# Writing the turned query weights back in the third row block of the next group, in 2 KB pieces, with the order of all lists written anew

## The reference, cut to what matters

```python
x = x + attn(layernorm(x), Wq, Wk, Wv, Wo, q_norm_w, k_norm_w)   # 32 heads, causal, alibi, q and k RMS-normalised
x = x + ffn(layernorm(x), A, B, Wr, br)                          # softmax router over 8 low-rank experts
# attn, per group g: q = x Wq[g].T, k = x Wk[g].T, v = x Wv[g].T
# scores = q k.T / sqrt(128) + slope * rel (causal); p = softmax(scores); o = p v; y += o Wo[:, g].T
```

## Time and profile before

| | |
|---|---|
| median of 3 runs | 2138.23 us (2137.99 to 2138.62) |
| the profiled execution's own time | 2138.16 us |
| its span, first to last instruction | 2136.3 us |
| granted PE clock, mean | 0.993 of full speed |
| PE busy | 2083.0 us, 98% of the span |
| DVE, ACT, POOL busy | 63%, 54%, 44% |
| DMA | 176.81 MB, mean 83 GB/s |
| queue of SP, queue of ACT | 72.41 MB in 305264 packets, 102.25 MB in 23664 |

### The profile page before, as it was taken

How to read it: one execution, slowest core, us unless ns; L and a number is a source line. 1 busy time by engine, 2 the same in 40 slices (tenths; PEclk the granted TensorE clock), 3 DMA queues, 4 the chain that set the end, 5 groups by cost and what they waited for, 6 DMA issues and landing times.

```text
span 2136.3 us, 33509 instructions
## 1 busy us (share of the span) xinstructions
PE 2083.0 (98%) x11772; PEld 1786.4 (84%) x11772; DVE 1355.6 (63%) x3431; ACT 1148.2 (54%) x3314; POOL 936.1 (44%) x984
## 2 busy tenths in 40 slices
PE   7999999999999999999999999999999999999997
PEld 6888888888888888888888888888888888888885
DVE  6656656566565665658876556566566656656676
ACT  4555545555454654645445555555555555555552
POOL 3443434444444443444443544435453443545443
PEclk9999999999999999999999999999999999999998
DMA  4152141511415125051350422313041231304112
GB/s 158 64 140 75 30 130 64 154 60 40 133 54 150 60 55 157 16 154 55 110 157 7 113 70 68 101 50 92 28 107 62 67 102 50 89 30 106 44 36 73
DMA packets 329095, 176.81 MB, mean 83 GB/s; under 512 B 243800, under 2 KB 301144, under 8 KB 320736
## 3 DMA queue, kind: packets, MB, share of 16 engines
q1 hardware_dynamic: 305264, 72.41, 15.3%
q10 hardware_dynamic: 23664, 102.25, 12.8%
HBM read 99.11 MB, written 75.50 MB: 82 GB/s over the span
## 4 chain that ended last, share of the span: by engine, by line
PE 83%; DVE 4%; issue 4%; DMA 3%; SPq 2%; POOL 2%; ACT 2%; ACTq 0%; DVEq 0%; POOLq 0%
PE s_ps L1026 17%; PE q_ps L1026 15%; PE y_ps L1026 15%; PE o_ps L1026 15%; PE turn_ps L1113 13%; PE turn_ps L1026 5%; DMA p_raw<-p_bounce 3%; SPq L568 2%; POOL probs_odd L799 1%; PE turn_ps L1107 1%; PE y_ps L1186 1%; DVE pT_lo L898 1%; DMA p_bounce<-probs_odd 1%; DVE y L955 0%; DVE oT_lo L949 0%
## 5 line engine op out<-in xcount | busy, mean ns | idle before, releaser
L799 POOL TENSOR_TENSOR probs_odd<-probs_odd,p_inv 128x256 f32<-128x256 f32 (+3 forms) x256 | 316.4, 1256 | 326.9 <-DVE p_inv L928 326.9
L706 ACT ACTIVATE pT_hi<-turn_ps 128x512 fp32r<-128x512 f32 x464 | 271.6, 597 | 316.2 <-PE turn_ps L1113 315.9
L799 POOL TENSOR_TENSOR probs_even<-probs_even,p_inv 128x128 f32<-128x128 f32 (+3 forms) x256 | 261.8, 1044 | 386.1 <-DVE p_inv L928 386.1
L898 DVE TENSOR_TENSOR pT_lo<-turn_ps,pT_hi 128x512 fp32r<-128x512 f32 x464 | 314.6, 684 | 146.2 <-ACT pT_hi L706 145.2
L921 DVE CUSTOM_DVE_ANT_0 probs_odd<-s_ps,rel 128x256 f32<-128x256 f32 (+3 forms) x256 | 209.3, 820 | 131.9 <-issue 131.4
L1026 PE MATMUL s_ps<-kT_hi,qT_hi 128*128 128x512 f32 (+3 forms) x768 | 278.7, 363 | 2.6 <-DVE kT_lo L900 1.8
L1026 PE MATMUL s_ps<-kT_hi,qT_lo 128*128 128x512 f32 (+3 forms) x768 | 262.9, 342 | 0.0
L1026 PE MATMUL s_ps<-kT_lo,qT_hi 128*128 128x512 f32 (+3 forms) x768 | 262.1, 341 | 0.0
L720 ACT ACTIVATE probs_odd<-probs_odd,neg_max 128x256 f32<-128x256 f32 (+3 forms) x256 | 211.9, 832 | 76.0 <-DVE neg_max L921 75.9
L921 DVE CUSTOM_DVE_ANT_0 probs_even<-s_ps,rel 128x128 f32<-128x128 f32 (+3 forms) x256 | 174.0, 686 | 118.0 <-issue 117.2
L1026 PE MATMUL o_ps<-pT_hi,v_hi 128*128 128x512 f32 x576 | 243.9, 423 | 1.9 <-DVE pT_lo L898 0.9
(11 more groups left out here) (110 smaller groups left out, 4578.6 us busy)
## 6 DMA issues: line engine op xcount, KB each, us to landing
p_raw<-p_bounce SPq DMA_DIRECT2D x448, 64.0 KB, 2.3
p_bounce<-probs_odd SPq DMA_DIRECT2D x64, 256.0 KB, 2.3
wq_kept<-wqT_hi ACTq DMA_DIRECT2D x8, 1024.0 KB, 5.8
wq_kept<-wqT_lo ACTq DMA_DIRECT2D x8, 1024.0 KB, 8.4
wo_kept<-woT_hi ACTq DMA_DIRECT2D x8, 1024.0 KB, 8.1
wo_kept<-woT_lo ACTq DMA_DIRECT2D x8, 1024.0 KB, 10.2
p_bounce<-probs_even SPq DMA_DIRECT2D x64, 128.0 KB, 1.8
wqT_hi<-wq_kept ACTq DMA_DIRECT2D x8, 1024.0 KB, 4.8
```

The source lines that it names most:

```text
L706: nc.scalar.activation(target, bank, ACT.Copy).then_inc(sems["high"], 1)
L799: nc.gpsimd.tensor_tensor(row, row, p_inv[:, s % 2, h:h + 1].to_broadcast((P, L)), ALU.mult).then_inc(sems["normalise"], 1)
L898: nc.vector.tensor_tensor(target, bank, upper.bitcast(F32), ALU.subtract).then_inc(sems["low"], 1)
```

## The change

Three things are edited. The kept copies of all turned weights get another layout in HBM, in which a run is 2 KB rather than 8 KB (4 KB for the keys' and values'). `keep_wq(w)` now means the weights of group w itself. And all six lists are replaced by others with the same operations; only `keep_wq` leaves `PROLOGUE` and is added to `BOUNDARY`. The order of the operations on every engine changes with them, in many places. In `GROUP_A` the DMA issues stand so:

| issue on ACT's queue | before, behind | after, behind |
|---|---|---|
| `load_wq` | `max.2.1` | `max.2.3` |
| `keep_wq` | `values.7.1` | `scores.4.0` (ACT: `high.p.2.2`) |
| `load_wkv` | `flip_p.6.6` | `max.4.2` |
| `keep_wo` | `exp.2.0` | `values.4.3` (ACT: `square_q.7`) |
| `load_wo` | `high.p.7.1` | `normalise.6.2` (ACT: `high.p.5.4`) |
| `keep_wkv` | `values.7.3` | `turn.k.0` (ACT: `upper_p.7.6`) |

```diff
-        wq_kept = nc.dram_tensor("wq_kept", [NG, 2, P, C * W512], F32).ap()
+        wq_kept = nc.dram_tensor("wq_kept", [NG, 2, C, P, W512], F32).ap()
...
+        def pieces(kept, g, part):
+            return kept[g, part].rearrange("c p n -> p c n")
+
+        def pairs(turned):
+            return turned[:].rearrange("p (a c) n -> p a (c n)", c=2).bitcast(F32)
...
             def keep_wq(w):
-                after(act, "low", "wq", w + 1, C - 1)
-                act.dma_start(wq_kept[w + 1, 0], wqT_hi[:].rearrange("p c n -> p (c n)").bitcast(F32)).then_inc(wq_spilled, 16)
-                act.dma_start(wq_kept[w + 1, 1], wqT_lo[:].rearrange("p c n -> p (c n)").bitcast(F32)).then_inc(wq_spilled, 16)
+                after(act, "low", "wq", w, C - 1)
+                act.dma_start(pieces(wq_kept, w, 0), wqT_hi[:].bitcast(F32)).then_inc(wq_spilled, 16)
+                act.dma_start(pieces(wq_kept, w, 1), wqT_lo[:].bitcast(F32)).then_inc(wq_spilled, 16)
```

`keep_wo`, `keep_wkv` and the three `back_` functions are changed in the same way. The end of `GROUP_A` after:

```diff
+    "fetch_p.7.5 values.6.3 add_y.5 values.6.4 fetch_p.7.6 values.6.5 turn.p.7.0 values.6.6 high.p.7.0 turn.p.7.1 "
...
+    "values.7.4 flip_p.7.7 values.7.5 upper_p.7.6 turn.k.0 keep_wkv lower_p.7.6 y.6 upper_p.7.7 high.k.0 lower_p.7.7 "
```

More of the change, by code:

```diff
@@ L480, in x_normed @@
             return x_source(b, t)
-        wkv_kept = nc.dram_tensor("wkv_kept", [NG, 2, P, C * 2 * HD], F32).ap()
-        wq_kept = nc.dram_tensor("wq_kept", [NG, 2, P, C * W512], F32).ap()
-        wo_kept = nc.dram_tensor("wo_kept", [NG, 2, P, G * DM], F32).ap()
+        wkv_kept = nc.dram_tensor("wkv_kept", [NG, 2, C // 2, P, W512], F32).ap()
+        wq_kept = nc.dram_tensor("wq_kept", [NG, 2, C, P, W512], F32).ap()
+        wo_kept = nc.dram_tensor("wo_kept", [NG, 2, G, P, DM], F32).ap()
+        def pieces(kept, g, part):
+            return kept[g, part].rearrange("c p n -> p c n")
+        def pairs(turned):
+            return turned[:].rearrange("p (a c) n -> p a (c n)", c=2).bitcast(F32)
         p_bounce = nc.dram_tensor("p_bounce", [2, NT, G, P, P], F32).ap()
@@ L630, in keep_wkv @@
                 after(act, "low", "wkv", w + 1, 1)
-                act.dma_start(wkv_kept[w + 1, 0], wkvT_hi[:].rearrange("p c n -> p (c n)").bitcast(F32)).then_inc(wkv_spilled, 16)
-                act.dma_start(wkv_kept[w + 1, 1], wkvT_lo[:].rearrange("p c n -> p (c n)").bitcast(F32)).then_inc(wkv_spilled, 16)
+                act.dma_start(pieces(wkv_kept, w + 1, 0), pairs(wkvT_hi)).then_inc(wkv_spilled, 16)
+                act.dma_start(pieces(wkv_kept, w + 1, 1), pairs(wkvT_lo)).then_inc(wkv_spilled, 16)
             def keep_wq(w):
-                after(act, "low", "wq", w + 1, C - 1)
-                act.dma_start(wq_kept[w + 1, 0], wqT_hi[:].rearrange("p c n -> p (c n)").bitcast(F32)).then_inc(wq_spilled, 16)
-                act.dma_start(wq_kept[w + 1, 1], wqT_lo[:].rearrange("p c n -> p (c n)").bitcast(F32)).then_inc(wq_spilled, 16)
+                after(act, "low", "wq", w, C - 1)
+                act.dma_start(pieces(wq_kept, w, 0), wqT_hi[:].bitcast(F32)).then_inc(wq_spilled, 16)
+                act.dma_start(pieces(wq_kept, w, 1), wqT_lo[:].bitcast(F32)).then_inc(wq_spilled, 16)
             def keep_wo(w):
                 after(act, "low", "wo", w, G - 1)
-                act.dma_start(wo_kept[w, 0], woT_hi[:].rearrange("p c n -> p (c n)").bitcast(F32)).then_inc(wo_spilled, 16)
-                act.dma_start(wo_kept[w, 1], woT_lo[:].rearrange("p c n -> p (c n)").bitcast(F32)).then_inc(wo_spilled, 16)
+                act.dma_start(pieces(wo_kept, w, 0), woT_hi[:].bitcast(F32)).then_inc(wo_spilled, 16)
+                act.dma_start(pieces(wo_kept, w, 1), woT_lo[:].bitcast(F32)).then_inc(wo_spilled, 16)
             def back_wkv(w):
@@ L647, in back_wkv @@
                 act.wait_ge(wkv_spilled, 32 * NG)
-                act.dma_start(wkvT_hi[:].rearrange("p c n -> p (c n)").bitcast(F32), wkv_kept[g, 0]).then_inc(wkv_back, 16)
-                act.dma_start(wkvT_lo[:].rearrange("p c n -> p (c n)").bitcast(F32), wkv_kept[g, 1]).then_inc(wkv_back, 16)
+                act.dma_start(pairs(wkvT_hi), pieces(wkv_kept, g, 0)).then_inc(wkv_back, 16)
+                act.dma_start(pairs(wkvT_lo), pieces(wkv_kept, g, 1)).then_inc(wkv_back, 16)
             def back_wq(w):
@@ L654, in back_wq @@
                 act.wait_ge(wq_spilled, 32 * NG)
-                act.dma_start(wqT_hi[:].rearrange("p c n -> p (c n)").bitcast(F32), wq_kept[g, 0]).then_inc(wq_back, 16)
-                act.dma_start(wqT_lo[:].rearrange("p c n -> p (c n)").bitcast(F32), wq_kept[g, 1]).then_inc(wq_back, 16)
+                act.dma_start(wqT_hi[:].bitcast(F32), pieces(wq_kept, g, 0)).then_inc(wq_back, 16)
+                act.dma_start(wqT_lo[:].bitcast(F32), pieces(wq_kept, g, 1)).then_inc(wq_back, 16)
             def back_wo(w):
@@ L661, in back_wo @@
                 act.wait_ge(wo_spilled, 32 * NG)
-                act.dma_start(woT_hi[:].rearrange("p c n -> p (c n)").bitcast(F32), wo_kept[g, 0]).then_inc(wo_back, 16)
-                act.dma_start(woT_lo[:].rearrange("p c n -> p (c n)").bitcast(F32), wo_kept[g, 1]).then_inc(wo_back, 16)
+                act.dma_start(woT_hi[:].bitcast(F32), pieces(wo_kept, g, 0)).then_inc(wo_back, 16)
+                act.dma_start(woT_lo[:].bitcast(F32), pieces(wo_kept, g, 1)).then_inc(wo_back, 16)
             def high(w, of, *which):
```

## The result

The kernel after takes 2108.43 us (median of 4 runs, 2108.18 to 2110.02); the kernel before, run beside it on the same chip, 2138.43 (2137.99 to 2139.65). The ratio is 0.986, 95% interval 0.9843 to 0.9877: 30.0 us less. The forecast was 25.1 less, 2113.1.

The account below looks back on a forecast made before the run. PE, busy 98% of the span, bounds the kernel; only its idle time and slow clock can be won. 25.4 - 1.0 + 1.5 - 0.8 = 25.1 us less than 2138.16 gives 2113.1 us, range 2105 to 2127.

Parts of the forecast that it names:

- Step 1, the six A periods: GROUP_A periods: y.6 no longer waits for add_y.5 behind slow fetches; 131.4 to 127.9 us each, 21.0 us saved.
- Either edit alone would take this wait away: Moving the transfers, or moving add_y.5 ahead of row 7's flips, would each end y.6's wait in GROUP_A.
- the fourth rival: Flip's place on DVE, not the collision, caused the wait; same 25 us gain, chance included in the forecast's 0.74.
- Step 1, group 0: Group 0, ahead of the first y.7: wait of 2.6 and slow product's 1.8 give 4.4 us saved.
- Step 2, what is late next in A: Values 7.7 have some 3 us slack; thinner places in the seven A groups cost 1 us, bounds 0 to 7.
- Step 3, the issues that moved: keep_wq about 34 us into the group, keep_wo at 67, load_wo at 80: their new places cost nothing.
- Step 4, pieces of 2 KB: Kept copies in 2 KB runs: charged 0, bounds 0 to 2 us a group of batch 1.
- Step 5, batch 1 and the seams: Six GROUP_B periods save 1.5 us at y.7; prologue, boundary, first batch 1 and last groups lose 0.8, bounds -5 to +5.
- half of it: Row 7 chain late at the A groups' end, PE waits about 1.8 us each: 2126 us, chance 0.13.
- moved, not removed: keep_wo and load_wo meet the fetch of tile 5.5, giving back 25 us: 2138 us, chance 0.05.
- slower for another reason: Row 7 fetches stay at 8 to 9 us from their own 128-byte reads; values 7.7 wait: 2151 us, chance 0.04.

Follow-up runs that it names:

- e2: Kernel before with only keep_wq moved to row block 3 (dropped from the prologue, added to the boundary group), 8 KB runs: 2111.92 us, ratio 0.9874.
- e1: Kernel before with only its kept copies laid out in 2 KB pieces, every order list unchanged: 2140.14 us, ratio 1.001.
- e4: Kernel before with only add_y.5 moved on DVE, ahead of flip_p.7.4, all transfers in place: 2139.63 us, ratio 1.0007.
- e7: Kernel after with keep_wq put back at the group's end, behind upper_p.7.4, for the next group's weights: 2114.39 us, ratio 0.9886.
- e6: Kernel after with its kept copies back in 8 KB runs, all order lists as after: 2108.90 us, ratio 0.9861.
- e8: Kernel after with add_y.5 put back behind flip_p.7.6 on DVE: 2108.53 us, ratio 0.9858.
- e10: Kernel before with keep_wq moved one ACT entry later, behind upper_p.7.4, 8 KB runs: 2146.71 us, ratio 1.0039.

## Why the prediction was right, and where its sizes were off

The profiled executions give 28.1 where the sum gave 25.1. By the steps:

- *Step 1, the six A periods.* Right, and the seven groups run at a granted clock of 1.00 (first row; the second is the last group, where the 1.00 that I forecast to the end fails, at 0.96 for 0.95 before over its own stretch):

```profile
40.50:934.90 894.40, 894.40 (x5153) 775.96 (x5153) 580.01 (x1386) 518.79 (x1462) 393.78 (x399) 1.00 0.32 92
...
1960.70:2108.00 147.30, 132.05 (x685) 106.49 (x683) 101.35 (x291) 64.27 (x179) 59.11 (x68) 0.96 0.21 54
```

PE is busy in every one of the 894.4 us. The sizes: 21.8 us against 21.0, the period 127.8 against 127.9. The mechanism held in both directions: e2 takes the collision away and has no wait of `y.6`; e1 and e4 keep the collision and are no faster than the kernel before. Failed in one clause: "Either edit alone would take this wait away." It takes the wait of `y.6` away, but with the transfers in place (e4) the flip of 7.7 holds `norm_k` and the time doesn't change. So the fourth rival, that the flip's place was the reason, is wrong as well. The upper bound of this step was added up wrongly: with 3.5 us for the ten blocks it is 6 x 3.9 + 4.4 = 27.8, not 27.5. The 28.1 measured for the six periods and group 0 together lie above both, because of the next term.
- *Step 1, group 0.* The term mis-sized: 4.4 forecast, 6.3 measured. I took only the wait and the slow product at its end, and these were right: from the start of `y.0` to that of `y.7` group 0 takes 171.22 - 55.94 = 115.3 us before and 164.91 - 53.99 = 110.9 after, 4.4 less. All of the missing 1.9 lies ahead of `y.0`. The chains of the kernel before, e2 and the kernel after have it at:

```profile
55.94 2.76 PE y_ps L1026 x12
...
54.68 2.76 PE y_ps L1028 x12
...
53.99 2.77 PE y_ps L1035 x12
```

e2 has the order on PE of the kernel before and a clock of 1.00 where that has 0.82: 1.3 us. The other 0.7 came with the new prologue and order. I had no row for this stretch.
- *Step 2, what is late next in A.* Charged 1 us, measured nothing: all six periods are 127.7 to 127.8, and the view of PE's waits is empty from 165 to 931 us. The fetches take 1.9 to 3.5 us where I had 2.0 to 2.5, and the slack that I read at `values.7.7` covers it. e7 shows how near the edge is: once these fetches take up to 5.7 us, PE waits for `pT_lo` by up to 1.4, and two of the six periods are 129.4 and 129.5.
- *Step 3, the issues that moved.* Right. In group 5 `keep_wq` is issued at 710.73, 32 us behind the end of the last product of group 4 (675.88 + 2.75 in the chain), for 34 in my sums, and `load_wo` at 756.66, 78 for 80. The six fetches issued from 754.0 to 763.8 land in 1.9 to 2.4 us, and the flip of 5.5 (761.29) follows its neighbour on DVE without a gap.
- *Step 4, pieces of 2 KB.* Right at 0 for the time: e1 is 0.1% slower with an interval that just excludes none, e6 equal to the kernel after. The second half of `back_wo` takes 8.2 us in the median for 7.1 in 8 KB runs, where I allowed 3.6 more for 2 MB; in group 11 it is in at 1473.2, 5.8 us ahead of `y.0`. That shorter packets would make the remaining collision cheap, as I read the rule of the DMA rings, is not borne out: e1.
- *Step 5, batch 1 and the seams.* Forecast 1.5 - 0.8 = 0.7 less, measured 0.0 from the last `y.7` of A to the end, and neither term came, so that two misses partly cancel. The groups at the seams cost nothing: boundary, first group of batch 1 and last group take 147.3, 130.9 and 149.9 us before, 146.7, 131.0 and 150.1 now. The six `GROUP_B` periods take 748.7 before and 748.9 now instead of 1.5 less. The piece of `y.7` did shrink, 2.76 for 3.03 to 3.07, but the period stayed at 124.7 (1583.78 - 1459.04): the 0.3 came back inside the group. A product of the scores waits for a row maximum there. It starts 0.49 us behind the product ahead of it, where the spacing is otherwise 0.23, and the next one 0.34 behind it; the same gap stands in three more periods (at 1421.46, 1670.99 and 1795.82), and none in the two periods of the kernel before read at the same place. In the chain at 1546:

```profile
1546.11 0.10 DVE neg_max L930
1546.21 0.04 issue
1546.25 1.65 PE s_ps L1035 x6
```

The 0.0 is that of one execution: in e6, e7 and e8, which have the same list for the last group, it takes 148.9, 148.5 and 148.5 us instead of 150.1. That fits the 1.6 us by which the profiled execution lies above its median; what makes the last group vary is open.

So 0.8 (periods) + 1.9 (group 0) + 1.0 (step 2) - 0.7 (step 5) = 3.0 us more than forecast. Of the rivals, "half of it" is ruled out by the waits at the end of the A groups, which are not there; "moved, not removed" by the fetches of 5.5, which land in time; "slower for another reason" by the fetches at 2.4.

## What to carry to other kernels

When a wait ends at a small DMA that is slow in one place and fast in another, list what the other queues have in flight at both places before touching the waiting engine: here one entry of an order list, moved to where the small queue is empty, gave 26 of 30 us (with its counterpart moved from the prologue to the boundary group), while moving the waiting instruction and cutting the packets gave none. Moving half of the bytes gave nearly all, and moving them 2 us the wrong way cost 8 us: count from the first issue of the small transfers to their landing, not to their issue. What the whole rewrite of six lists added beyond that one entry is 3.5 us of 2138, and even this is not clear of the noise: the intervals of the two ratios overlap (0.9859 to 0.9888 and 0.9843 to 0.9877).

## What the runs showed of the hardware

- Where a fetch and a large transfer on another queue both have packets waiting, these go one for one, at 8 KB (205 to 219 in 4 us) as at 2 KB (547 to 554 in 3 us), and the fetch takes 8 us either way: it lands half a microsecond or less behind the large transfer (818.1 and 817.6; 820.4 and 820.2).
- Such a stream also stretches the issue of the fetches on SP's queue, from 0.49 us to as much as 1.4 to 2.7 us each, and a fetch can meet a transfer that is issued after it (10.1 us in e10 for one that starts 1.2 us ahead of `keep_wq`).
- A PE wait of 1.8 us ahead of group 0 was followed by a mean clock of 0.82 over the next 9.6 us in five profiles and by 1.00 in three, with the same order on PE up to there.
